# Cross scores of a row's four groups issued as one call over four banks, with the gated loop's order written out by hand

## The chip, the cores and the metric

The program runs on one core of a Trainium2 chip. The time is device time in microseconds, as the median of several executions. The range over which the executions before the change spread is given below, with the profiled execution's own time.

## The reference, cut to what matters

Sixteen rows of 128 tokens with 256 features pass through four layers: a memory layer with a gate, a layer with self attention, cross attention and two experts, and two layers of media attention with feed-forward. The change is in the attention part of the second layer. There each row has 16 heads for self attention (16 features a head, causal) and 16 heads for cross attention (8 features a head, no mask):

```python
def sdpa(q, k, v, causal):
    scale = 1.0 / np.sqrt(q.shape[-1])
    scores = jnp.einsum('bhqd,bhkd->bhqk', q * scale, k)
    ...
    p = jax.nn.softmax(scores.astype(jnp.float32), axis=-1).astype(q.dtype)
    return jnp.einsum('bhqk,bhkd->bhqd', p, v)
ctx = sdpa(q, k, v, causal=True)
hidden_states = residual + jnp.where(vm, ctx @ v_dense, ctx @ l_dense)
ci = rms_norm(hidden_states, ln_post_cross_w)
cctx = sdpa(cq, ck, cv, causal=False)
hidden_states = hidden_states + cctx @ cdense_w
```

## The kernel before, in words

**Units and passes.** The 16 rows are worked in 4 iterations of two units, A (0) and B (1), with two rows each. The second layer's attention is "phase 1". It is software-pipelined: a loop body that runs 3 times (called a pass here) holds the cross attention of this iteration and the self attention of the next. Before the first pass stands a prologue, and after the last one a drain whose order (`ORDER[2]`) is written out, and which overlaps the rounding of the experts' weights.

**Steps.** A step is named kind.attention.unit.row.group, as `scores_cross.cross.0.1.2`; a plus behind it means that it belongs to the next iteration. Every engine walks the same list of steps and runs its own part of each, in order. So a step's place in the list is its place in the queue of each engine that has a part in it. The text writes a step by kind, unit, row and group.

**Softmax of a group.** The 16 heads of a row are four groups of four heads, and the scores of a group (128 by 512) fill one PSUM bank. For one group: TensorE writes the scores, VectorE takes the row maxima (L1511), ScalarE takes the exponential from PSUM to an SBUF buffer with row sums (four activations, each with a read of its accumulator, L1774), VectorE takes reciprocals for two groups (L1518, step `share`), GpSimd multiplies two groups by them (L1994), TensorE transposes (step `turn`, L1021), VectorE copies the transposed bank to SBUF (L1406), and TensorE multiplies by the values (step `mix`, 128x32 column tiles).

**Cross scores.** The contraction of a group is over 32 partitions. One call of `scores_gated` issues two groups, on 32 rows of the array each and on one bank each. Self scores use 64 rows each, also two groups to a call, after two bf16 matmuls that write the causal mask.

**Banks.** All scores of phase 1 share banks 0 to 3, in rotation over the list. A row has four groups, so group g always lies in bank g. The mixes use bank 7, and all other steps (turns, xvT and xlT, qk, v1, dense and so on) rotate over banks 4 to 6. Before TensorE writes a bank it waits in `take` until the step that held it has been emptied. For scores this is the exponential, for xvT and xlT ScalarE's copy, for a turn VectorE's copy. These waits stand in TensorE's queue, and nothing behind one of them starts before it.

**Order.** The loop body's order comes from a table: `gated_slots()` lays the attention steps out in 16 slots, and `gated_sides()` adds the projections. The four score calls of a unit's cross attention stand apart. Between the third (0.1.0) and the fourth (0.1.2) stand both `qk` steps, the longest steps on TensorE in the body.

**Row sums and maxima.** `nmax`, `rsum` and `rshare` have four slots, by group, for both rows.

Of the kernel before, what the change touches and what calls it, by code (L numbers as in the profile page):

```python
# [30 lines left out]
P = 128  # L31
# [95 lines left out]

def gated_slots():
# [19 lines left out]
    for k in range(n):  # L148
        slots.append((of(k - 4, mix) + of(k - 3, lambda *pair: groups_of("turn", pair)),
                      of(k, lambda *pair: groups_of("scores", pair))  # L150
                      + of(k - 1, lambda *pair: groups_of("share", pair)[0:1])))
# [20 lines left out]

def gated_body():
    return [front + first + early + second + late
            for (first, second), (front, early, late) in zip(gated_slots(), gated_sides())]
# [108 lines left out]
def steps_self(norms, pre):  # L284
    slots = gated_body()
    if pre[0] == ("scale_self", A_):
        return [s for slot in slots for s in slot]
# [175 lines left out]
for _i in range(len(PLAN)):  # L463
# [9 lines left out]
        turn_cross.cross.0.0.0 scores_cross.cross.0.1.2 scores_cross.cross.0.1.3 share_cross.cross.0.1.0  # L473
        dense.1.0 round.experts.0 turn_cross.cross.0.0.1 dense.1.1 mix_cross.cross.0.0.0 norm_cross.1
        round.experts.1 turn_cross.cross.0.0.2 turn_cross.cross.0.0.3 split.experts.0 scale_cross.1
        share_cross.cross.0.1.2 mix_cross.cross.0.0.1 ck.1 coT.0.0 round.experts.2 split.experts.1
        turn_cross.cross.0.1.0 turn_cross.cross.0.1.1 nT.1 mix_cross.cross.0.1.0 finish.experts.0
        round.experts.3 turn_cross.cross.0.1.2 spread_cross.1.0 turn_cross.cross.0.1.3 cdense.0.0
        split.experts.2 half.0 mix_cross.cross.0.1.1 coT.0.1 cv.1 finish.experts.1 round.experts.4 cq.1
        spread_cross.1.1 split.experts.3 cdense.0.1 finish.experts.2 end.0 scores_cross.cross.1.0.0 norm_mlp.0  # L480
# [5 lines left out]
        turn_cross.cross.1.0.2 turn_cross.cross.1.0.3 split.experts.6 share_cross.cross.1.1.2 norm_mlp.1  # L486
# [3 lines left out]
        cdense.1.0 finish.experts.8 half.1 round.experts.11 split.experts.10 mix_cross.cross.1.1.1 cdense.1.1  # L490
        coT.1.1 finish.experts.9 end.1 split.experts.11 xvT2.0 xlT2.0 finish.experts.10 finish.experts.11
# [123 lines left out]
def build(nc, dram, out):  # L615
    with ExitStack() as ctx:
# [47 lines left out]
        rsum = sb("rsum", [P, P_RING, QUAD])  # L664
        rshare = sb("rshare", [P, P_RING, QUAD])
        pT_ring = [sb_twin(f"pT{i}", [P, BANK]) for i in range(PT_RING)]
        nmax = sb("nmax", [P, P_RING, QUAD])
# [196 lines left out]
        def settle(eng, name):  # L864

            eng.sem_inc(settled[name], 1)
# [139 lines left out]
        def _(pe):  # L1006
# [99 lines left out]

            def scores_gated(ph, it, s):
# [4 lines left out]
                banks = [ps[ph.bank[s[:4] + (g + i,)]] for i in range(2)]  # L1112
# [290 lines left out]
        def _(dve):  # L1403
# [105 lines left out]
            def scores(ph, it, s, bank):  # L1509
                dve.wait_ge(*after(ph, it, s, "mm"))  # L1510
                dve.tensor_reduce(nmax[:, s[4], :], bank[:, :].rearrange("p (h t) -> p h t", h=QUAD),  # L1511
                                       AX_X, ALU.max, negate=True).then_inc(sems[s[0], "max"], 1)

            def share(ph, it, s, bank):
# [3 lines left out]
                dve.reciprocal(rshare[:, g:g + 2, :], rsum[:, g:g + 2, :]).then_inc(sems[s[0], "rinv"], 1)  # L1518
# [189 lines left out]
        def _(act):  # L1708
# [49 lines left out]
            def scores(ph, it, s, bank):  # L1758
# [13 lines left out]
                for j in range(QUAD):  # L1772
                    part = slice(j * P, (j + 1) * P)
                    t = act.activation(p[:, part], bank[:, part], ACT.Exp, bias=nmax[:, g, j:j + 1],  # L1774
                                       accum_out=rsum[:, g, j:j + 1])
# [146 lines left out]
        def _(pool):  # L1922
# [65 lines left out]
            def share(ph, it, s, bank):  # L1988
# [3 lines left out]
                for n in range(2):  # L1992
                    p = p_of(s[:4] + (g + n,)).rearrange("q (h t) -> q h t", h=QUAD)
                    t = pool.tensor_tensor(p, p, rshare[:, g + n, :].unsqueeze(2).broadcast_to([P, QUAD, P]), ALU.mult)  # L1994
# [103 lines left out]
```

## Time and profile before

| | |
|---|---|
| median of 3 runs | 1407.32 us (1405.79 to 1413.47) |
| the profiled execution's own time | 1406.32 us |
| its span | 1404.1 us |
| what lies around the span | 2.2 us |
| one pass of the gated loop, from 236.88 to 324.97 | 88.09 us |
| TensorE busy in that pass | 86.18 us |
| ScalarE, GpSimd, VectorE busy in it | 57.35, 56.07, 55.85 us |
| the three passes | about 147 to 411 us |
| the drain | about 411 to 476 us |

Times in the profile count from the span's start. Engines: PE is TensorE, PEld its weight loads, DVE is VectorE, ACT is ScalarE, POOL is GpSimd. A float32 matmul is recorded as two matmuls with two weight loads, so two groups of cross scores give four records. A record's end is modelled. What a step costs TensorE is read from its start to the start of the step behind it.

### The profile page before, as it was taken

Reading aid. Unit: us, or ns where it says so; the run is one execution under the profiler, and the core shown is the slowest. Engines: PE = TensorE matmul, PEld = TensorE weight load, DVE = VectorE, ACT = ScalarE, POOL = GpSimd, SP = SyncE. Lnnn points to the kernel's source line nnn. Section 1 sums busy time; section 2 is a strip of 40 time slices with the busy share of each in tenths; the row PEclk is TensorE's granted clock in tenths of the full one; section 3 lists DMA queues with packets and bytes.
Section 4 is the critical chain, followed back from the end, with each engine's and each line's share of the span. In section 5 each row is a group of like instructions: output and inputs, shape, how many; then the busy total and the mean of one; then the engine's idle time right before and its main releaser. Section 6 shows DMA issues by size and latency. Waiting matters only on the chain.

```text
span 1404.1 us, 32336 instructions
## 1 busy us (share of the span) xinstructions
PE 1328.4 (95%) x10898; PEld 1102.9 (79%) x10898; DVE 868.3 (62%) x1837; ACT 755.1 (54%) x2861; POOL 435.8 (31%) x574
## 2 busy tenths in 40 slices
PE   7978999999997899999999999999989999998999
PEld 6844555555554799999888889889988888987999
DVE  4754566666665767548556666566666656556664
ACT  2333676566765722213866666663367665657422
POOL 1354666656664200000132333211013232323000
PEclk9999999999997799999999999999999999999999
DMA  5230000000000200000100000011001000000000
GB/s 180 81 129 4 5 5 5 4 0 4 4 1 1 99 1 0 0 1 1 62 9 5 4 4 4 0 35 64 0 1 65 6 4 4 7 0 1 9 22 30
DMA packets 13928, 30.33 MB, mean 22 GB/s; under 512 B 2832, under 2 KB 9488, under 8 KB 13200
## 3 DMA queue, kind: packets, MB, share of 16 engines
q1 hardware_dynamic: 13840, 29.23, 6.0%
q8 instruction: 46, 0.75, 0.2%
q14 instruction: 42, 0.34, 0.1%
HBM read 27.13 MB, written 2.10 MB: 21 GB/s over the span
## 4 chain that ended last, share of the span: by engine, by line
PE 74%; POOL 7%; DVE 6%; issue 6%; ACT 5%; SPq 1%; DMA 0%; POOLq 0%; DVEq 0%; ACTq 0%
PE bank L1008 65%; PE bank L1021 9%; POOL p L1994 2%; ACT p L1774 1%; POOL xn L1959 1%; DVE stats L1436 1%; POOL o L1994 1%; POOL kbd L1975 1%; DVE pT L1406 1%; DVE nmax L1511 1%; POOL kbd L1985 1%; POOL kbd L1994 1%; ACT kbd L1774 0%; DVE w_ff_rounded L1590 0%; DMA ctxT<-in_ctxT 0%
## 5 line engine op out<-in xcount | busy, mean ns | idle before, releaser
L1511 DVE TENSOR_REDUCE nmax<-bank 128x4 f32<-128x512 f32 x256 | 165.1, 685 | 97.9 <-PE bank L1008 96.7
L1406 DVE COPY pT<-bank 128x512 f32<-128x512 f32 x256 | 164.4, 681 | 90.9 <-PE bank L1021 90.7
L1008 PE MATMUL bank<-w_ff_rounded,hT_rounded 128*128 128x256 f32 x944 | 216.0, 284 | 4.2 <-ACT w_ff_rounded L1901 3.8
L1774 ACT ACTIVATE p<-bank,nmax 128x128 f32<-128x128 f32 x512 | 181.3, 397 | 70.0 <-DVE nmax L1511 69.8
L1994 POOL TENSOR_TENSOR p<-p,rshare 128x512 f32<-128x512 f32 x128 | 132.3, 1054 | 215.7 <-DVE rshare L1518 215.6
L1008 PE MATMUL bank<-xT_rounded,w_ff_rounded 128*128 128x256 f32 x864 | 196.1, 284 | 1.5 <-DVE xn_rounded L1573 1.5
L1008 PE MATMUL bank<-xn_rounded,w_ff_rounded 128*128 128x256 f32 x608 | 172.0, 283 | 0.0
L1008 PE MATMUL bank<-xT_rounded,kbd_rounded 128*128 128x256 f32 x608 | 171.9, 283 | 0.0
L1008 PEld LDWEIGHTS bank<-w_ff_rounded,hT_rounded 128*128 128x128 f32 x944 | 162.2, 191 | 5.4 <-issue 4.2
L1008 PEld LDWEIGHTS bank<-xT_rounded,w_ff_rounded 128*128 128x128 f32 x864 | 148.8, 192 | 2.1 <-DVE xn_rounded L1573 1.7
L1008 PE MATMUL bank<-kbd,hT 64*128 64x128 f32 (+2 forms) x1280 | 144.9, 354 | 4.4 <-ACT p L1774 3.7
L1711 ACT ACTIVATE o<-bank 128x512 f32<-128x512 f32 (+1 forms) x104 | 60.3, 582 | 145.2 <-PE bank L1008 133.2
L1008 PEld LDWEIGHTS bank<-pT,v 128*32 128x32 f32 (+1 forms) x2048 | 79.8, 124 | 66.4 <-issue 26.2
L1008 PE MATMUL bank<-pT,v 128*32 128x128 f32 (+1 forms) x2048 | 113.1, 283 | 18.0 <-DVE pT L1406 8.1
L1774 ACT ACTIVATION_READ_ACCUMULATOR p<-bank,nmax 128x1 f32 x512 | 120.6, 236 | 0.0
L1008 PEld LDWEIGHTS bank<-xn_rounded,w_ff_rounded 128*128 128x128 f32 x608 | 116.6, 192 | 0.0
L1008 PEld LDWEIGHTS bank<-xT_rounded,kbd_rounded 128*128 128x128 f32 x608 | 116.5, 192 | 0.0
L1008 PEld LDWEIGHTS bank<-kbd,hT 64*128 64x128 f32 (+1 forms) x1280 | 88.6, 190 | 26.9 <-issue 25.3
L1774 ACT ACTIVATE kbd<-bank,nmax 128x128 f32<-128x128 f32 x256 | 90.8, 403 | 29.0 <-DVE nmax L1511 29.0
L1008 PE MATMUL bank<-w_ff_rounded,o_rounded 128*128 128x256 f32 x352 | 99.5, 283 | 0.0
L1994 POOL TENSOR_TENSOR kbd<-kbd,rshare 128x512 f32<-128x512 f32 x64 | 65.7, 1047 | 92.8 <-DVE rshare L1518 92.8
L1629 DVE SCALAR_TENSOR_TENSOR x_all<-bank,tgates,x_all 128x256 f32 (+1 forms) x64 | 30.4, 481 | 98.2 <-PE bank L1008 98.1
(182 smaller groups left out, 3128.3 us busy)
## 6 DMA issues: line engine op xcount, KB each, us to landing
ctxT<-in_ctxT SPq DMA_DIRECT2D x32, 128.0 KB, 2.4
w_ff<-in_w1b SPq DMA_DIRECT2D x6, 640.0 KB, 6.4
w_att<-in_w2a SPq DMA_DIRECT2D x1, 3072.0 KB
w_att<-in_w3a SPq DMA_DIRECT2D x1, 3072.0 KB
w_att<-in_w1a SPq DMA_DIRECT2D x1, 2304.0 KB
hT<-in_xT SPq DMA_DIRECT2D x8, 256.0 KB, 3.1
o<-in_x SPq DMA_DIRECT2D x8, 256.0 KB, 2.8
w_ff<-in_w2b SPq DMA_DIRECT2D x1, 2048.0 KB, 7.6
```

Of the source, the lines that this page charges most:

```text
L1008: return pe.matmul(dst, lhsT, rhs, start=first, stop=last)
L1021: t = pe.transpose(bank[:, i * P:(i + 1) * P], src, ident[:])
L1406: dve.tensor_copy(dst, src).then_inc(sems[s[0], "copied"], 1)
L1436: t = dve.bn_stats(stats[:, u, b, :], of(b))
L1511: dve.tensor_reduce(nmax[:, s[4], :], bank[:, :].rearrange("p (h t) -> p h t", h=QUAD), AX_X, ALU.max, negate=True).then_inc(sems[s[0], "m ...
L1629: dve.scalar_tensor_tensor(out=x_b, in0=ps[ph.bank[job]][:, 0:D].unsqueeze(1), scalar=tgates[:, n:n + 1], in1=x_b, op0=ALU.mult, op1=ALU.a ...
L1711: act.activation(dst, src, func, scale=scale).then_inc(sems[s[0], event], 1)
L1774: t = act.activation(p[:, part], bank[:, part], ACT.Exp, bias=nmax[:, g, j:j + 1], accum_out=rsum[:, g, j:j + 1])
L1959: pool.tensor_tensor(xn[u][:, :, :, :], x_all[:, rows(it, u), :].unsqueeze(2).broadcast_to(to_all), rstd_in[:, rows(it, u), :].unsqueeze(3 ...
L1975: pool.tensor_tensor(w.k1[:, b, c, :, :], src.unsqueeze(1).broadcast_to([P, QUAD, P]), rows_self[:, :].unsqueeze(2).broadcast_to([P, QUAD, ...
L1985: pool.tensor_tensor(w.ck1[:, b, :, :], src.unsqueeze(1).broadcast_to([P, QUAD, P]), rows_cross[:, :].unsqueeze(2).broadcast_to([P, QUAD, ...
L1994: t = pool.tensor_tensor(p, p, rshare[:, g + n, :].unsqueeze(2).broadcast_to([P, QUAD, P]), ALU.mult)
```

## The change

1. All four groups of a row's cross scores are issued in one call: TensorE takes banks 0 to 3, one after another, and issues four matmuls on the array's rows 0, 32, 64 and 96. The steps of groups 1 to 3 do nothing on TensorE any more. VectorE and ScalarE still run one step for each group.
2. The loop body is no longer made from the table, but written out in `GATED_BODY`. It holds the same 156 steps in another order.
3. The drain's order `ORDER[2]` is changed at some places. Its cross score calls fall to the place of group 0 as well.
4. `nmax` and `rsum` get eight slots, by row and group. The reciprocal is taken in place, and `rshare` is gone.

```diff
+def scores_of(kind, u, b, c):
+    if kind == "self":
+        return groups_of("scores", (kind, u, b, c))
+    return [("scores_cross", kind, u, b, g) for g in range(GROUPS)] if c == 0 else []
...
+GATED_BODY = """
+    mix.self.1.0.0 scale_self.0+ turn.self.1.0.2 turn.self.1.0.3 scores_cross.cross.0.0.0 mix.self.1.0.1 ctx.1.0
+    scores_cross.cross.0.0.1 scores_cross.cross.0.0.2 scores_cross.cross.0.0.3 turn.self.1.1.0 turn.self.1.1.1
+    share.self.1.1.2 mix.self.1.1.0 xvT.0+ xlT.0+ share_cross.cross.0.0.0 scores_cross.cross.0.1.0
+    scores_cross.cross.0.1.1 scores_cross.cross.0.1.2 turn.self.1.1.2 scores_cross.cross.0.1.3 turn.self.1.1.3
+    qk.0.0+ qk.0.1+ mix.self.1.1.1 share_cross.cross.0.0.2 dense.1.0 ctx.1.1 turn_cross.cross.0.0.0
...
+    scores.self.0.1.1+ coT.0.1 share.self.0.0.2+ turn.self.0.0.0+ turn.self.0.0.1+ cv.1 spread_cross.1.1
+    scores.self.0.1.2+ scores.self.0.1.3+ cq.1 cdense.0.1 share.self.0.1.0+ scale_self.1+ mix.self.0.0.0+ end.0
+    turn.self.0.0.2+ scores_cross.cross.1.0.0 scores_cross.cross.1.0.1 turn.self.0.0.3+ scores_cross.cross.1.0.2
+    scores_cross.cross.1.0.3 share.self.0.1.2+ mix.self.0.0.1+ ctx.0.0+ turn.self.0.1.0+ turn.self.0.1.1+ xvT.1+
+    xlT.1+ mix.self.0.1.0+ share_cross.cross.1.0.0 turn.self.0.1.2+ turn.self.0.1.3+ scores_cross.cross.1.1.0
+    scores_cross.cross.1.1.1 scores_cross.cross.1.1.2 scores_cross.cross.1.1.3 qk.1.0+ qk.1.1+
...
+    cdense.1.0 half.1 coT.1.1 turn.self.1.0.0+ scores.self.1.1.2+ turn.self.1.0.1+ cq.0+ cv.0+
+    scores.self.1.1.3+ cdense.1.1 share.self.1.1.0+ end.1 spread_cross.0.1+"""
...
+            def at_once(s):
+                return GROUPS if s[1] == "cross" else 2
...
-                banks = [ps[ph.bank[s[:4] + (g + i,)]] for i in range(2)]
+                banks = [ps[ph.bank[s[:4] + (g + i,)]] for i in range(at_once(s))]
...
-                    if s[4] % 2 == 0:
-                        take(ph, it, s)
-                        settle(pe, "tensor")
-                        take(ph, it, s[:4] + (s[4] + 1,))
-                        settle(pe, "tensor")
+                    if s[4] % at_once(s) == 0:
+                        for i in range(at_once(s)):
+                            take(ph, it, s[:4] + (s[4] + i,))
+                            settle(pe, "tensor")
...
-                dve.reciprocal(rshare[:, g:g + 2, :], rsum[:, g:g + 2, :]).then_inc(sems[s[0], "rinv"], 1)
+                at = b * GROUPS + g
+                dve.reciprocal(rsum[:, at:at + 2, :], rsum[:, at:at + 2, :]).then_inc(sems[s[0], "rinv"], 1)
```

## Rows read from the trace of the kernel before

**Rows 1.** The page's first two parts: busy time, and the span in 40 slices.

```profile
PE 1328.4 (95%) x10898; PEld 1102.9 (79%) x10898; DVE 868.3 (62%) x1837; ACT 755.1 (54%) x2861; POOL 435.8 (31%) x574
...
PEclk9999999999997799999999999999999999999999
```

**Rows 2.** Busy time by stretch: stretch, its length, each engine's busy time (instructions), granted clock, DMA.

```profile
236.88:324.97 88.09, 86.18 (x613) 49.23 (x612) 55.85 (x117) 57.35 (x292) 56.07 (x60) 1.00 0.01 3
...
412.00:476.00 64.00, 50.53 (x356) 29.81 (x352) 43.08 (x95) 41.72 (x182) 28.87 (x39) 0.73 0.02 6
...
417.30:420.70 3.40, 2.07 (x25) 0.87 (x23) 2.66 (x6) 3.40 (x21) 2.60 (x3) 1.00 0.02 5
...
420.00:430.00 10.00, 10.00 (x54) 4.92 (x55) 4.93 (x10) 6.69 (x38) 4.14 (x5) 0.54 0.00 1
```

**Rows 3.** PE in order of time, a pass's start: start, length, instructions, idle before and releaser.

```profile
238.78 1.13 PE L1008 MATMUL bank<-kbd,hT 32*128 32x512 f32 x4
239.84 0.65 PE L1008 MATMUL bank<-pT,v 128*32 128x128 f32 x16
240.41 1.09 PE L1021 MATMUL bank<-consts,kbd 128*128 128x128 f32 x8
241.91 1.09 PE L1021 MATMUL bank<-consts,xn 128*128 128x128 f32 x8 [0.40 <-POOL xn L1959]
242.93 1.13 PE L1008 MATMUL bank<-kbd,hT 32*128 32x512 f32 x4
244.06 0.64 PE L1008 MATMUL bank<-pT,v 128*32 128x128 f32 x16
244.64 1.09 PE L1021 MATMUL bank<-consts,o 128*128 128x128 f32 x8
245.66 1.13 PE L1008 MATMUL bank<-kbd,hT 32*128 32x512 f32 x4
246.72 7.13 PE L1008 MATMUL bank<-w_att,xT 128*128 128x512 f32 x16
```

**Rows 4.** The same view of DVE.

```profile
236.35 1.29 DVE L1511 TENSOR_REDUCE nmax<-bank 128x4 f32<-128x512 f32 x2 [2.11 <-PE bank L1008]
...
239.91 1.29 DVE L1511 TENSOR_REDUCE nmax<-bank 128x4 f32<-128x512 f32 x2 [0.43 <-PE bank L1008]
```

**Rows 5.** The same view of ACT.

```profile
237.08 0.37 ACT L1774 ACTIVATE o<-bank,nmax 128x128 f32<-128x128 f32 x1 [1.64 <-DVE nmax L1511]
...
239.74 0.24 ACT L1774 ACTIVATION_READ_ACCUMULATOR o<-bank,nmax 128x1 f32 x1
...
243.59 0.42 ACT L1786 ACTIVATE hT<-bank 128x256 f32<-128x256 f32 x1
243.85 1.62 ACT L1741 ACTIVATE xT<-bank,consts 128x256 f32<-128x256 f32 x4
...
246.66 0.47 ACT L1774 ACTIVATE p<-bank,nmax 128x128 f32<-128x128 f32 x1
...
248.03 0.50 ACT L1774 ACTIVATE kbd<-bank,nmax 128x128 f32<-128x128 f32 x1
...
249.40 0.53 ACT L1774 ACTIVATE kbd<-bank,nmax 128x128 f32<-128x128 f32 x1
```

**Rows 6.** The same view of POOL.

```profile
239.96 1.90 POOL L1959 TENSOR_TENSOR xn<-x_all,rstd_in 128x1024 f32 x1
241.81 2.04 POOL L1994 TENSOR_TENSOR o<-o,rshare 128x512 f32<-128x512 f32 x2
```

**Rows 7.** PE in order of time, ahead of the first pass and in the drain.

```profile
146.65 0.59 PE L1008 MATMUL bank<-causal,ident 128*128 128x512 bf16 x2
147.17 1.13 PE L1008 MATMUL bank<-kbd,hT 64*128 64x512 f32 x4
...
149.83 1.13 PE L1008 MATMUL bank<-kbd,hT 32*128 32x512 f32 x4
...
453.34 2.08 PE L1008 MATMUL bank<-kbd,hT 32*128 32x512 f32 x4 [3.71 <-ACT p L1774]
```

**Rows 8.** ACT in the drain, the record that ends an exponential's bank.

```profile
452.83 0.21 ACT L1774 ACTIVATION_READ_ACCUMULATOR p<-bank,nmax 128x1 f32 x1
```

More of the change, by code:

```diff
@@ L149, in gated_slots @@
         slots.append((of(k - 4, mix) + of(k - 3, lambda *pair: groups_of("turn", pair)),
-                      of(k, lambda *pair: groups_of("scores", pair))
+                      of(k, scores_of)
                       + of(k - 1, lambda *pair: groups_of("share", pair)[0:1])))
@@ L173, in gated_body, with step @@
 def gated_body():
-    return [front + first + early + second + late
-            for (first, second), (front, early, late) in zip(gated_slots(), gated_sides())]
+    def step(text):
+        return tuple(int(x) if x.isdigit() else x for x in text.rstrip("+").split("."))
+    return [[(step(text), int(text.endswith("+"))) for text in GATED_BODY.split()]]
 def media_slots():
@@ L285, in steps_self @@
     slots = gated_body()
-    if pre[0] == ("scale_self", A_):
+    if ("scale_self", A_) in pre:
         return [s for slot in slots for s in slot]
@@ L489 @@
         finish.experts.7 turn_cross.cross.1.1.2 round.experts.10 turn_cross.cross.1.1.3 split.experts.9
-        cdense.1.0 finish.experts.8 half.1 round.experts.11 split.experts.10 mix_cross.cross.1.1.1 cdense.1.1
-        coT.1.1 finish.experts.9 end.1 split.experts.11 xvT2.0 xlT2.0 finish.experts.10 finish.experts.11
+        cdense.1.0 finish.experts.8 xvT2.0 xlT2.0 half.1 round.experts.11 split.experts.10 finish.experts.9
+        mix_cross.cross.1.1.1 cdense.1.1 coT.1.1 end.1 split.experts.11 finish.experts.10 finish.experts.11
         round.experts.12 round.experts.13 split.experts.12 round.experts.14 split.experts.13 finish.experts.12
@@ L663, in build @@
         p_ring = [sb_twin(f"p{i}", [P, BANK]) for i in range(P_RING)]
-        rsum = sb("rsum", [P, P_RING, QUAD])
-        rshare = sb("rshare", [P, P_RING, QUAD])
+        rsum = sb("rsum", [P, ROWS * GROUPS, QUAD])
         pT_ring = [sb_twin(f"pT{i}", [P, BANK]) for i in range(PT_RING)]
-        nmax = sb("nmax", [P, P_RING, QUAD])
+        nmax = sb("nmax", [P, ROWS * GROUPS, QUAD])
         rows_self = sb("rows_self", [P, QUAD])
@@ L1510, in scores @@
                 dve.wait_ge(*after(ph, it, s, "mm"))
-                dve.tensor_reduce(nmax[:, s[4], :], bank[:, :].rearrange("p (h t) -> p h t", h=QUAD),
+                dve.tensor_reduce(nmax[:, s[3] * GROUPS + s[4], :], bank[:, :].rearrange("p (h t) -> p h t", h=QUAD),
                                        AX_X, ALU.max, negate=True).then_inc(sems[s[0], "max"], 1)
@@ L1773, in scores @@
                     part = slice(j * P, (j + 1) * P)
-                    t = act.activation(p[:, part], bank[:, part], ACT.Exp, bias=nmax[:, g, j:j + 1],
-                                       accum_out=rsum[:, g, j:j + 1])
+                    t = act.activation(p[:, part], bank[:, part], ACT.Exp, bias=nmax[:, b * GROUPS + g, j:j + 1],
+                                       accum_out=rsum[:, b * GROUPS + g, j:j + 1])
                 t.then_inc(sems[s[0], "exp"], 1)
```

31 lines of the change are left out of this document (22 added, 9 removed).

## The prediction

> **What bounds the kernel now.** I read the page first: TensorE is busy 95% of the span [rows 1], so an instruction saved there can count. Then busy time by stretch, for the stage that the change touches. In one pass of the gated loop TensorE works 86.18 of 88.09 us, and no other engine more than 57.35 [rows 2]. The pass is bound by TensorE's queue, with little waiting. The three passes take 3 x 88.1 = 264 us of 1404. The drain is another matter: TensorE is busy 50.53 of 64.00 us, and the granted clock is 0.73 on average [rows 2], so latency between engines sets its time. Then I read each engine in order of time to price steps and chains [rows 3 to 8]. The reader should look for starts: the step behind a cross score call starts 1.06 us after it (238.78 to 239.84, 245.66 to 246.72).
>
> **What is removed on TensorE.** Two groups of cross scores cost 1.06 us. One record of a 512-column float32 matmul costs TensorE 0.44 (16 records in the 7.0 us of the two qk steps [rows 3]). Four in turn would be 1.8, so the two groups already run side by side, and what is paid is one group's two records (0.87) plus 0.2 for filling and draining the array at the change of tile. If four groups run as two do, the call costs hardly more: I take 1.07. Bounds: 1.06 if the other two are free, 2.12 if the array takes them two by two.
>
> A pass has eight calls before and four after, so 4 x 1.05 = 4.2 us go. Where the neighbours of a removed call are both 128-row work, they now follow without a drain of the array. A turn of four transposes takes 0.49 behind another kind of tile and 0.44 behind its own kind. Summing all steps of a pass by their start-to-start distances, those of rows 3 and like ones for the rest, and leaving waits out, gives 84.9 us before and 80.2 after: **-4.7 us a pass**. The pass before thus has 88.1 - 84.9 = 3.2 us of waits. Two of its waits are for xn from GpSimd (0.40 in rows 3, at 241.91).
>
> If all waits stayed as they are, the passes would give 3 x 4.7 = 14 us back.
>
> The Trainium skill, "TensorE: Matmul & The Clock Gate", Part 3, gives a measured speedup of 3.07 for four row tiles of 32 rows with 512 columns. By it, as an estimate, the call would take (4 x 0.87 + 0.2) / 3.07 = 1.2 us, and the calls would save 3.6 us a pass, not 4.2. No run here shows four tiles yet.
>
> **What is added: a wait for all four banks.** A call with two groups needs two banks empty, and the other two may still be in ScalarE's hands. A call with four needs all of them. Only ScalarE's last exponential frees bank 3. So between two calls of a unit lies the full latency of four exponentials. I walk it from the first call's start, Q:
> - VectorE's first maximum starts at Q + 1.13 (238.78 to 239.91 [rows 3, 4]).
> - ScalarE's first exponential starts 0.73 later (236.35 to 237.08 [rows 4, 5]), at Q + 1.9. The maxima come every 0.6 us (two in 1.29 [rows 4]), faster than ScalarE uses them.
> - One bank's exponentials take 1.37 us from start to start (246.66, 248.03, 249.40 [rows 5]), and the last ends about 1.5 after its start. Two banks took 237.08 to 239.98. Four end at Q + 1.9 + 3 x 1.38 + 1.5 = Q + 7.5.
> - The new order puts ctx.1.0 between the first and second (0.26 from start to start, 243.59 to 243.85 [rows 5]): Q + 7.8.
> - TensorE needs another 0.3 us through its waits once the bank is free: in the drain an exponential's last record ends at 453.04 [rows 8], and the call that waited for it starts at 453.34, after 3.71 us of idling [rows 7]. This is the wait that now comes into the loop.
>
> So unit A's second call can't start before **Q + 8.1**. What TensorE has to do between the two calls in the new list is the first call, mix, two turns, mix, xvT and xlT: 1.07 + 0.58 + 1.02 + 0.58 + 1.02 = 4.3 us. **Wait: 3.8.** The 7.0 us of qk, which could cover it, stand behind the call. Within these 3.8 us one wait is only moved: VectorE takes four maxima ahead of the copies of turns 1.1.0 and 1.1.1, so the mix behind them starts at Q + 5.0 and not Q + 2.7.
>
> Unit B's second call: the four exponentials end at R + 7.5, then come in ScalarE's queue ctx.0.0 (0.26) and xvT.1's two copies (0.8 to 0.9, half of 243.85 to 245.28 [rows 5]), at R + 8.6. Turn 0.1.3 stands ahead of the call and takes the bank that xvT.1 held, so it starts at 8.7, and the call at R + 9.2. TensorE's work between is 5.7. **Wait: 3.5.**
>
> Unit B's first call waits for self group 0.1.3 and then for cq.1's copy, which the new list puts behind it on ScalarE. From the start of the self call 0.1.2: 0.53 for the mask [rows 7], 1.13 to the maximum, 0.73 to the exponential, 1.38 + 1.5 for two banks, 0.45 for cq's copy, 0.3 to start: 6.0. TensorE's work between is 4.2. **Wait: 1.8.** Unit A's first call waits for self group 1.1.3, whose exponential stands behind the copies of cq.0 and cv.0: it ends 5.9 us after its call's start, so the wait, 0.3 to start included, is **0.5** over 5.6 us of work.
>
> The rest of the pass I walked in the same way. Four small waits come out: dense.1.1 for its bank from dense.1.0 (0.3), ck.1 for that of turn 0.1.0 (0.4), turn 1.1.3 for nT.0's (0.2), and self call 1.1.2 for GpSimd's spread (0.2). GpSimd's shares of 2.04 us and its xn of 1.90 [rows 6] arrive in time, because the waits at the calls give it time.
>
> Sum of waits: 3.8 + 3.5 + 1.8 + 0.5 + 1.1 = 10.7 us against 3.2, **+7.5 a pass**. Net of the work saved: **+2.8 a pass, +8.3 in three**. The walk has some 60 joints. I give it 1.5 us a pass to either side.
>
> "TensorEngine Tiling (Array Packing)" of the Trainium skill, Performance Considerations, says that tiling speeds TensorE but not the emptying of PSUM, which may then bound. By that rule the saving would shrink. The rows above put ScalarE in that place, in two stretches of a pass only: over the whole pass it is 57 of 88 us busy.
>
> **Into the first pass.** Before, the first cross call starts 3.2 us after self call 1.1.2 (146.65 to 149.83 [rows 7]), with two banks long free. After, it waits for the exponential of 1.1.3, at + 5.9: **+2.7**. No earlier step has the slack to give this back, since the prologue's steps hang on each other.
>
> **The drain.** Four calls fewer at half clock (2.08 each [rows 7]) are 8 us of TensorE's work, but its time is set by the chain of exponentials. Unit A: the first call comes 1.9 us later (it waits for 1.1.3), and the last exponential some 1.8 earlier, as it no longer waits for the fourth call. Unit B: 3.71 us of idling stood before the third call already, and it grows by two exponentials, while the fourth call's wait goes. I take **0**, from -3 to +2. The moved steps of `ORDER[2]` go by at most three places, and their work (a copy or a rounding of 0.4 to 0.7 us) lies beside these waits.
>
> **The clock.** From 417.3 to 420.7 TensorE was busy 2.07 of 3.40 us, with waits for ScalarE. After this the granted clock was half (1.2 GHz in place of 2.4) for most of 420 to 430 [rows 2]. In the three passes it was never below full. After the change, TensorE works some 1.6 of the 5.5 us up to unit A's second call, and about half of a like stretch in unit B. So I expect the clock to fall about once a pass. While it is low, the work (turns, the call, a part of qk) takes double. Bounds: 0, and 3.5, if in both units a quarter of the 7 us of qk behind the second call still runs at half clock. I take 1.2 a pass, **+3.6**, since a part of each lies in the waits.
>
> **nmax, rsum and the reciprocal in place** change addresses. The reciprocals (0.2 us) stay as many. A maximum that had to wait for a slot would show here, but no wait of that kind stood in the code. Cost: 0. No DMA is added or moved: the queue on SP waits for cv and ck of the same pass, with nearly a pass of room.
>
> **Sum.** 8.3 + 2.7 + 0 + 3.6 = +14.6 on the profiled execution's own 1406.3 (span 1404.1) gives 1420.9. The median shown is 1 us above it. I round down to **1420**, as the clock's share is the least sure.
>
> **The rivals.**
> - *The work saved comes through (0.19).* If ScalarE frees the four banks in time, waits stay at about 3 us a pass, and the time is 1406 - 14 - 2 = **1390**. For it: 95% TensorE, 20 to 30 us of slack a pass on the others. Against: it needs four exponentials within 4.3 us, where four take 5.6. It decides itself at unit A's second call: if it starts before Q + 5.5, this rival holds.
> - *Saving and waits cancel (0.10).* My walk is 2 us a pass too dark, as some waits get covered, and the clock holds: **1408**, within 1401 to 1414.
> - *Four tiles don't run side by side (0.07).* The call then takes 2.1. As all four calls start late, most of the 1.05 us each is added: 12 passes' calls and 4 in the drain, some +14 over the forecast: **1434**.
> - *The forecast (0.64)*, with its own range of 1411 to 1429. One sixth of it lies below 1414.4.
>
> **How the numbers follow.** Half a per cent, 7 us, is about what a measurement of this kernel can tell from no change: 1400.3 and 1414.4 are the bounds. Faster: 0.18, nearly all of the first rival. Same: 0.20, the second rival and the lower edge of the forecast. Slower: 0.62. The range goes from 1396, inside the faster rival's upper tail, to 1431, short of the fourth case.
>
> **What the profile after would show.** Four-group calls of 1.07 us from start to start, with eight records. A PE idle time before unit A's second call (together with the mix before it) of 3 to 4 us, put down to ScalarE's exponential. From first to second call about 8.1 us in A and 9.2 in B. A pass of about 91 to 92 us with TensorE busy some 81, and half-clock stretches in it. I would be wrong if a pass is under 88 us: then look whether the second call starts before its row's third bank has been emptied, or the exponentials run faster than 1.37 us a bank.

## The result, and the profile after

The changed kernel takes 1428.35 us in the median (1425.35 to 1429.98, 4 runs), beside 1408.97 us for the kernel before (1405.79 to 1413.47, 4 runs): a ratio of 1.016 with a 95% interval of 1.0122 to 1.0197 (the quotient of the two medians alone is 1.014). It is slower, by 19 us between the medians and 24 between the two profiled executions. The forecast was 1420 us, within 1396 to 1431: the sign and the range hold. The size does not: 14.6 us were added up for the profiled execution, and it lost 23.7. The profiled execution took 1429.98 us, span 1427.8.

The page's first two parts answer to [rows 1]:

```profile
PE 1318.5 (92%) x10898; PEld 1106.1 (77%) x10898; DVE 874.6 (61%) x1837; ACT 756.5 (53%) x2861; POOL 434.3 (30%) x574
...
PEclk9989999999999799999999999999999999999999
```

TensorE is busy 10 us less than before, and the kernel takes 24 us more. Busy time by stretch, as in [rows 2]: the three passes of the gated loop, each from unit A's first cross call to the next, and the drain up to the first matmul of the MLP.

```profile
154.01:247.95 93.94, 83.38 (x612) 48.96 (x613) 57.70 (x117) 57.84 (x292) 55.97 (x61) 0.98 0.01 4
247.95:344.05 96.10, 85.94 (x612) 50.62 (x613) 57.70 (x117) 57.84 (x292) 55.96 (x61) 0.95 0.01 3
344.05:439.79 95.74, 86.11 (x612) 51.19 (x613) 57.60 (x117) 57.84 (x292) 55.87 (x61) 0.95 0.01 2
439.79:498.09 58.30, 37.52 (x327) 24.52 (x327) 41.03 (x92) 39.57 (x167) 26.10 (x37) 0.82 0.00 1
```

A pass took 88.1 us and takes 94 to 96, and the granted clock, 1.00 in a pass before, is 0.95 to 0.98. The starts of the same TensorE steps in the two traces split the 23.7 us of span:

| part | before | after | difference | forecast |
|---|---|---|---|---|
| start of the first cross call | 149.83 | 154.01 | +4.2 | +2.7 |
| three passes | 265.0 | 285.8 | +20.8 | +8.3, and +3.6 for the clock |
| drain, to the MLP's first matmul | 61.5 | 58.3 | -3.2 | 0 |
| the rest of the kernel | 927.8 | 929.7 | +2.0 | 0 |

TensorE in order of time, the second pass's start (it answers to [rows 3]), and below the dots unit B's calls in the same pass:

```profile
247.95 1.14 PE L1046 MATMUL bank<-kbd,hT 32*128 32x512 f32 x8 [0.57 <-ACT o L1816]
249.02 0.64 PE L1046 MATMUL bank<-pT,v 128*32 128x128 f32 x16
249.60 1.09 PE L1059 MATMUL bank<-consts,kbd 128*128 128x128 f32 x8
252.86 0.64 PE L1046 MATMUL bank<-pT,v 128*32 128x128 f32 x16 [2.17 <-issue]
253.44 1.50 PE L1059 MATMUL bank<-consts,xn 128*128 128x128 f32 x8
256.25 2.09 PE L1046 MATMUL bank<-kbd,hT 32*128 32x512 f32 x8 [1.31 <-ACT p L1816]
258.27 1.97 PE L1059 MATMUL bank<-consts,o 128*128 128x128 f32 x8
...
296.80 1.14 PE L1046 MATMUL bank<-kbd,hT 32*128 32x512 f32 x8 [1.50 <-ACT hT L1753]
...
299.87 0.64 PE L1046 MATMUL bank<-pT,v 128*32 128x128 f32 x16 [1.34 <-DVE pT L1447]
...
304.76 0.74 PE L1046 MATMUL bank<-pT,v 128*32 128x128 f32 x16 [2.15 <-ACT hT L1828]
305.43 1.97 PE L1059 MATMUL bank<-consts,o 128*128 128x128 f32 x8
307.33 1.74 PE L1046 MATMUL bank<-kbd,hT 32*128 32x512 f32 x8
```

Three things are to be seen. The call of four groups has eight records and costs 1.07 us (247.95 to 249.02), what the call of two cost. TensorE now idles ahead of three of the four calls and ahead of the mixes between two calls. The releasers are ScalarE's exponentials and copies in four of these six waits, VectorE's copy in one (299.87), and none is named in one (252.86). And at 256.25 the work takes about double: the same call 2.02, the record of the two turns behind it 1.97 in place of 1.09.

ScalarE in order of time, the first and the last exponential between unit A's two calls, answers to [rows 5]:

```profile
249.89 0.37 ACT L1816 ACTIVATE p<-bank,nmax 128x128 f32<-128x128 f32 x1 [2.32 <-DVE nmax L1552]
...
255.31 0.46 ACT L1816 ACTIVATE p<-bank,nmax 128x128 f32<-128x128 f32 x1
255.56 0.30 ACT L1816 ACTIVATION_READ_ACCUMULATOR p<-bank,nmax 128x1 f32 x1
```

From Q, the start of unit A's first call (247.95), the first starts at Q + 1.94, the last ends at Q + 7.91, and the call starts 0.39 later, at Q + 8.30. The walk had 1.9, 7.8 and 8.1.

VectorE in order of time (it answers to [rows 4]) shows the other wait:

```profile
249.08 2.48 DVE L1552 TENSOR_REDUCE nmax<-bank 128x4 f32<-128x512 f32 x4 [0.81 <-PE bank L1046]
251.48 1.28 DVE L1447 COPY pT<-bank 128x512 f32<-128x512 f32 x2
```

Four maxima stand ahead of the copies of the two turns. The mix that needs these copies starts at 252.86, Q + 4.9 (the walk: 5.0), and the profile names no releaser for its 2.17 us.

### The profile page after: what moved, and what is told of

Its sections match the earlier page's. It is cut to its first block, busy times and chain, and to the rows that moved or that the text cites. A ratio compares the mean times of both kernels' runs of the same rounds, so it can differ in the third digit from the quotient of the medians.

```text
span 1427.8 us, 32323 instructions
## 1 busy us (share of the span) xinstructions
PE 1318.5 (92%) x10898; PEld 1106.1 (77%) x10898; DVE 874.6 (61%) x1837; ACT 756.5 (53%) x2861; POOL 434.3 (30%) x574
## 4 chain that ended last, share of the span: by engine, by line
PE 75%; ACT 9%; DVE 8%; issue 4%; POOL 2%; SPq 1%; DMA 0%; DVEq 0%; ACTq 0%; POOLq 0%
PE bank L1046 66%; PE bank L1059 9%; ACT p L1816 4%; DVE nmax L1552 2%; ACT o L1816 1%; DVE stats L1477 1%; DVE pT L1447 1%; ACT kbd L1816 1%; DVE x_all L1582 1%; DMA ctxT<-in_ctxT 0%; ACT v L1753 0%; DVE w_ff_rounded L1632 0%; POOL kbd L2017 0%; POOL rstd L1983 0%; SPq L969 0%
## 5 line engine op out<-in xcount | busy, mean ns | idle before, releaser
L2036 POOL TENSOR_TENSOR p<-p,rsum 128x512 f32<-128x512 f32 x128 | 132.3, 1054 | 211.6 <-DVE rsum L1560 211.6
L1046 PE MATMUL bank<-kbd,hT 64*128 64x128 f32 (+2 forms) x1280 | 128.0, 363 | 17.9 <-ACT p L1816 11.2
L1046 PEld LDWEIGHTS bank<-kbd,hT 64*128 64x128 f32 (+1 forms) x1280 | 84.6, 193 | 38.1 <-issue 36.5
L2036 POOL TENSOR_TENSOR kbd<-kbd,rsum 128x512 f32<-128x512 f32 x64 | 65.8, 1048 | 83.9 <-DVE rsum L1560 83.7
```

Source lines behind the costliest of these rows:

```text
L1046: return pe.matmul(dst, lhsT, rhs, start=first, stop=last)
L2036: t = pool.tensor_tensor(p, p, rsum[:, s[3] * GROUPS + g + n, :].unsqueeze(2).broadcast_to([P, QUAD, P]), ALU.mult)
```

## The experiments

All are timed beside the kernel before on the same chip. Its medians there were 1407.45 us (12 runs) for the first four experiments, 1406.45 (31 runs) for the next four, 1403.0 (29 runs) for the three tries further, and 1408.39 (13 runs) for the last. The ratios and intervals given are not quotients of two medians. Pass lengths are from unit A's first call to the next.

**The order alone.** The changed kernel, with calls of two groups.

```diff
             def at_once(s):
-                return GROUPS if s[1] == "cross" else 2
+                return 2
```

> The changed kernel with its new order, but cross score calls of two groups again. Theory (waits for the banks, and the clock falls that they bring): the new list puts the two calls of a row side by side, so the call for groups 2 and 3 of the second row still waits for the first row's last exponential, 8.1 us after the first call. TensorE does 4.2 us more work a pass, most of it inside these waits: 1421 to 1430 us, a pass of 93 to 96 us. Rival (the four-group call itself is slow on the array or on the banks): the time falls clearly, to 1412 or less, since that call is gone.

1414.55 us (1413.60 to 1418.80, 9 runs), ratio 1.0069 (1.0044 to 1.0095). A pass is 92.1 us, with the clock low for 6.8 us in it; the drain is 52.9. The number lies between the two expectations, and the wait that was expected for the last call hardly shows: it starts 8.26 us after the first call, after an idle time of 0.13 us only. The new order costs the loop 4 us a pass by itself. TensorE is busy 87.76 of the 92.11 us, so 2.4 us of the 4 are more waits than before (4.35 against 1.9), and 1.6 are work at half clock. The maxima still stand ahead of the turns' copies (the mix waits 1.57 us), and the copies ahead of unit B's call (1.5). The calls of four add 3.2 us a pass to that.

**Calls of four alone.** The calls of four in the lists of the kernel before, for the loop and the drain.

```diff
-GATED_BODY = """ ... """
 def gated_body():
+    return [front + first + early + second + late
+            for (first, second), (front, early, late) in zip(gated_slots(), gated_sides())]
```

> Calls of four groups, with the loop's and the drain's order of the kernel before. Theory (waits for the banks): in the old order the second call of a unit stands even nearer, and the copies of xvT and xlT stand between the exponentials, so it starts 9.6 us after the first, over 5.2 us of work, and the first call of a unit waits for the last self exponential (1.8). Pass 95 us without and 97 with falls of the clock: 1428 to 1440 us. Rival (the new order is at fault, not the call of four): the work saved shows, 1390 to 1400 us.

1439.98 us (1437.02 to 1442.28, 4 runs), ratio 1.0251 (1.0195 to 1.0306); a pass of 99.0. TensorE's waits in the second pass (total, times, longest):

```profile
PE bank L1043 <- ACT p L1813: 5.8, 2, 2.9
PE bank L1043 <- ACT o L1813: 5.0, 3, 1.8
PE bank L1043 <- ACT hT L1825: 2.7, 2, 1.4
PE bank L1043 <- ACT hT L1832: 0.8, 2, 0.4
```

In the same order with calls of two, TensorE's waits in a pass were these:

```profile
PE bank L1021 <- POOL xn L1959: 1.1, 2, 0.7
PE bank L1008 <- ACT hT L1793: 0.8, 2, 0.4
```

None was for an exponential; now they are 10.8 us of a pass. The time lies at the upper edge of what was expected, and the pass is 2 us longer than the 97 expected. So the wait comes with the calls of four, and the new order takes off some of it: of the four combinations the pass is 88.1 (old, two), 99.0 (old, four), 92.1 (new, two), 95.3 (new, four, mean of three).

**The clock.** The changed kernel, with transposes repeated into a bank that the turn holds anyway, so that TensorE works where it waited. They add 52 transposes a pass and leave the results as they are.

```diff
+            AGAIN = {("turn", "self", 1, 1, 0): 2, ("turn", "self", 1, 1, 1): 1, ("xlT", 0): 4,
+                     ("turn", "self", 0, 0, 3): 1, ("xlT", 1): 5}
...
+                    for i, src in blocks_and_places:
+                        pe.transpose(bank[:, i * P:(i + 1) * P], src, ident[:])
```

> The changed kernel, where in the passes TensorE repeats transposes of five turns inside its waits (same data, same bank, before anybody is told). It adds 5.7 us of TensorE's work a pass, in places where it idles, so as to keep the clock up. Theory (the falls of the clock cost 3 to 4 us a pass): no or few stretches at half clock in the passes, and 1417 to 1422 us. Rival (the low clock falls into waits and costs nearly nothing): the clock stays up, and the time stays within 3 us of 1428, or grows if the added work delays a copy.

1420.09 us (1419.37 to 1420.27, 4 runs), ratio 1.0109 (1.0057 to 1.0162). Busy time of the second pass:

```profile
244.09:336.40 92.31, 87.37 (x665) 53.94 (x665) 57.62 (x117) 57.71 (x292) 55.91 (x61) 1.00 0.01 3
```

TensorE does more, and the kernel is 8.3 us faster than the changed one by the medians. These were taken beside two different runs of the kernel before, whose medians differ by 1.5 us, so 7 to 8 us are safe. The clock is full in all three passes, and they take 92.3 us each: 276.8 in all, 8.9 less than in the changed kernel. The distance from first to second call is 8.28 in unit A, as before the repeats, so it was not the clock that set that one; in unit B it is 9.55, where it was 10.1 to 10.8.

**A copy earlier in unit B.** mix.self.0.0.1 and ctx.0.0 stand right behind turn 0.0.3, so that ScalarE's copy does not stand behind four exponentials.

```diff
-    ... turn.self.0.0.3+ scores_cross.cross.1.0.2 scores_cross.cross.1.0.3 share.self.0.1.2+ mix.self.0.0.1+ ctx.0.0+ ...
+    ... turn.self.0.0.3+ mix.self.0.0.1+ ctx.0.0+ scores_cross.cross.1.0.2 scores_cross.cross.1.0.3 share.self.0.1.2+ ...
```

> The changed kernel with one move: unit B's mix.0.0.1 and ctx.0.0 stand before groups 2 and 3 of its first row, so ScalarE copies ctx.0.0 between the second and third exponential and not behind the fourth. Theory (the mix of row 1 waits for this copy, as all mixes hold bank 7, and pushes the second call from 9.2 to 10.5 us behind the first): the second call comes at 9.2 us, the pass loses 1.3 to 2 us, and the time is 1422 to 1425. Rival (the second call is held by the exponentials and the xvT copy alone): no change, 1427 to 1429.

1421.68 us (1421.23 to 1424.38, 4 runs), ratio 1.0121 (1.0069 to 1.0173). The time comes out just under what was expected, and for another reason. The wait of 2.15 us at 304.76 is gone, but one of 1.48 us for a copy of xT stands a step later, and the second call still starts 9.5 us after the first, as in the run of the repeated transposes. What the run gains on the changed kernel is clock. Its first two passes:

```profile
152.57:244.98 92.41, 82.18 (x613) 48.28 (x613) 57.72 (x117) 57.84 (x292) 55.50 (x61) 1.00 0.01 4
244.98:340.51 95.53, 85.33 (x612) 49.66 (x613) 57.72 (x117) 57.84 (x292) 55.96 (x61) 0.96 0.01 3
```

Same list, same code: 92.4 us at full clock and 95.5 with 6.8 us at half. This gives the clock's price a second time, and without added work.

**The second call behind qk.** In the changed kernel's list unit A's second call is placed behind qk.0.0 and unit B's behind qk.1.0, and the copies ctx, xvT, xlT between the first and the second exponential. Some neighbours move too: the shares, the turns ahead of the second calls, and in unit B the self call 0.1.2, which now stands ahead of turn.0.0.0. The cut shows unit A.

```diff
-    share.self.1.1.2 mix.self.1.1.0 xvT.0+ xlT.0+ share_cross.cross.0.0.0 scores_cross.cross.0.1.0 ...
-    qk.0.0+ qk.0.1+ ...
+    ... xvT.0+ xlT.0+ scores_cross.cross.0.0.1 scores_cross.cross.0.0.2 scores_cross.cross.0.0.3 mix.self.1.1.0 ...
+    share_cross.cross.0.0.0 qk.0.0+ scores_cross.cross.0.1.0 ... scores_cross.cross.0.1.3 qk.0.1+ ...
```

> The changed kernel with its calls of four, but in the loop's list the second cross call of unit A stands behind the step qk.0.0 and that of unit B behind qk.1.0 (3.5 us of TensorE's work each, now between the two calls in place of behind them); share.1.1.2, ctx, xvT and xlT are placed so that ScalarE's queue holds fewer copies between the exponentials. Theory (the calls of four save their work, and only the wait for four exponentials ate it): the work between the calls is now 7.8 us or more, so the waits of 3.8 and 3.5 us go and with them the falls of the clock; a pass of 85 to 87 us, 1396 to 1404 us in all. Rival (ScalarE's exponentials cost their time wherever the call stands, and their lateness only shows at the next step): the pass stays at 91 us or more and the time at 1412 or more.

> The same move as in the run before, in unit A alone; unit B as in the changed kernel. Theory: unit A's wait of some 4 us goes and unit B's stays. 3.5 us of work are now under the exponentials in each of three passes, and the falls of the clock at unit A (about 1.2 us a pass) go too: a pass of 90 to 92 us and 1412 to 1417 us in all, half of the way to the run with both. Rival (the wait moves from A to B's call, as a pass has one fixed total of latency): as the changed kernel, 1425 or more.

Both units: 1407.72 us (1406.21 to 1408.86, 10 runs), ratio 1.0003 (0.9984 to 1.0022). Unit A alone: 1414.92 us (1413.76 to 1415.37, 10 runs), ratio 1.0059 (1.0039 to 1.0078). The second is as expected. The first falls between the two expectations: all of the loss is gone, and no gain comes. Busy time of its second pass, and TensorE in order of time:

```profile
240.22:328.42 88.20, 82.36 (x612) 48.05 (x613) 57.65 (x117) 57.45 (x292) 56.01 (x61) 1.00 0.01 3
```

```profile
243.98 0.64 PE L1046 MATMUL bank<-pT,v 128*32 128x128 f32 x16
244.86 1.09 PE L1059 MATMUL bank<-consts,o 128*128 128x128 f32 x8 [0.24 <-POOL o L2036]
245.79 3.60 PE L1046 MATMUL bank<-w_att,xT 128*128 128x512 f32 x8
249.97 1.14 PE L1046 MATMUL bank<-kbd,hT 32*128 32x512 f32 x8 [0.58 <-ACT p L1816]
```

The mix of 2.17 us's wait has none now, since one maximum and not four stands ahead of its copies, and the second call waits 0.58 in place of 1.31, at full clock. But the call starts 9.75 us after the first (240.22), not 8.3: ScalarE now has xT's copies too, 1.4 us, among the four exponentials. TensorE is busy 3.8 us less than in the pass before (86.18 [rows 2]) and waits 3.9 us more (5.8 against 1.9): saving and waits cancel.

**Short exponentials.** One instruction of ScalarE for each cross bank. It leaves out each head's own maximum and three of the four row sums.

```diff
+                if kind == "cross":
+                    t = act.activation(p[:, :], bank[:, :], ACT.Exp, scale=0.001, accum_out=rsum[:, at, 0:1])
-                for j in range(QUAD):
+                for j in range(QUAD if kind != "cross" else 0):
```

> The changed kernel with its list, but each cross group is exponentiated by one ScalarE instruction of 512 columns in place of four of 128 (without each head's own maximum, and with one row sum where there are four: this leaves a part of the computation out). This shortens only ScalarE's part of the chain that empties the banks, from 1.37 us a bank to an estimated 0.6. Theory (the four exponentials set the second call): the second call starts at about Q + 5.3 in unit A, where VectorE's four maxima now set it, in place of Q + 8.3; a pass of 85 to 88 us; with a shorter drain too, 1385 to 1400 us in all. Rival (the wait is not ScalarE's but the turns' and copies' on VectorE, or the taking of four banks one by one): first to second call stays at 7.5 us or more and the pass at 91 or more.

1401.7 us (1399.59 to 1405.32, 10 runs), ratio 0.9972 (0.9945 to 0.9999); a pass of 88.6. Both are a little above what was expected, and clearly below the rival's 91 us a pass. TensorE in order of time:

```profile
241.08 1.14 PE L1046 MATMUL bank<-kbd,hT 32*128 32x512 f32 x8 [0.57 <-ACT o L1819]
...
245.99 0.64 PE L1046 MATMUL bank<-pT,v 128*32 128x128 f32 x16 [2.17 <-issue]
246.56 1.09 PE L1059 MATMUL bank<-consts,xn 128*128 128x128 f32 x8
247.59 1.14 PE L1046 MATMUL bank<-kbd,hT 32*128 32x512 f32 x8
```

With ScalarE's part short, the second call comes 6.5 us after the first (8.3 in the changed kernel, 5.3 expected) and waits for nothing, and the clock stays full in all three passes. The mix waits its 2.17 us as before, so that wait is VectorE's four maxima and not an exponential. Two causes stand one behind the other here, and the walk had both.

**Eight slots alone.** The kernel before, with the new nmax and rsum and the reciprocal in place.

> The kernel before, with only the change of nmax and rsum to eight slots and the reciprocal written in place. Theory: no cost and no gain, 1404 to 1411 us, as forecast (0). Rival (the four slots shared by two rows made VectorE or GpSimd wait): some us faster, 1400 or less.

1408.76 us (1400.63 to 1411.25, 10 runs), ratio 1.0017 (0.9988 to 1.0046); a pass of 88.05. No cost that can be told from nothing, as forecast.

**Three tries further.** To the second calls behind qk, mix.self.1.1.1 and mix.self.0.1.1 moved ahead of the second calls and dense.0.1 moved back; then the drain in calls of two with that; and the new list of the drain in the kernel before.

```diff
-    ... qk.0.0+ scores_cross.cross.0.1.0 ... qk.0.1+ mix.self.1.1.1 ...
+    ... qk.0.0+ mix.self.1.1.1 scores_cross.cross.0.1.0 ... qk.0.1+ ...
```

```diff
-            def at_once(s):
-                return GROUPS if s[1] == "cross" else 2
+            def at_once(s, it):
+                return GROUPS if s[1] == "cross" and not isinstance(it, int) else 2
```

> The kernel with the second calls behind qk.0.0 and qk.1.0 (pass 88.2 us, of it 5.9 us of waits), with three steps moved more: mix.self.1.1.1 and mix.self.0.1.1 between qk and the second call (0.58 us of work each, where that call still waits 0.58 and 0.67 us), and dense.0.1 behind mix_cross.1.0.0 (it waits 1.36 us for a copy of ScalarE). Theory (a call of four costs nothing once as much work as four exponentials take stands between two calls): about 2.5 us of waits go, a pass of 85.7 us and 1397 to 1404 us in all, faster than both kernels. Rival (a pass has 8 us of latency that only moves from wait to wait): pass 88 or more, 1406 or more.

> The same, but the drain behind the loop takes its cross scores in calls of two. There is no qk to stand between two calls there: unit B's second call waited 7.0 us. The run of calls of two with the new order had a drain of 52.9 us from the first call to the first matmul of the MLP, against 56.4 with calls of four and 61.5 in the kernel before. Theory: the drain takes 53 us, 3.5 us less than with calls of four: 1393 to 1401 us in all. Rival (the drain's time is the order's and not the calls'): no difference to the run before this one.

> The loop and the calls of two of the kernel before; only the new list of the drain (and the eight slots for maxima and sums). Theory (forecast before: the moved steps of the drain are worth nothing, since they lie beside waits): no change, 1404 to 1410 us, with the drain at 61 us. Rival (the new list is what made the drain shorter): drain of 53 to 55 us, 1398 to 1403 us in all.

The first took 1408.91 us (1406.58 to 1415.80, 12 runs), ratio 1.0042 (1.0015 to 1.0069), where 1397 to 1404 was expected: a miss. Its second pass is 88.2 us, no shorter. TensorE in order of time:

```profile
247.65 3.60 PE L1046 MATMUL bank<-w_att,xT 128*128 128x512 f32 x8
251.18 0.64 PE L1046 MATMUL bank<-pT,v 128*32 128x128 f32 x16
252.38 1.14 PE L1046 MATMUL bank<-kbd,hT 32*128 32x512 f32 x8 [0.55 <-issue]
```

The mix took 0.58 us of work out of the wait, and the call came 10.3 us after the first in place of 9.75. The last exponential's record ends at 251.43, so 0.95 us pass before the call; behind qk it was 0.39. dense.0.1 waited 1.35 us at its new place too. The pass has 6.0 us of waits, where it had 5.8. The rival holds: the waits moved.

The second took 1405.3 us (1402.49 to 1410.01, 12 runs), ratio 1.0011 (0.9987 to 1.0036), 3.6 us below the first, the 3.5 that were expected; the level is missed with that of the first. The drain is 52.9 us in its profile and 58.3 in that of the first, so the calls of four do lengthen it in this list.

The third, the kernel before with the new drain, took 1406.68 us (1397.96 to 1411.05, 12 runs), ratio 1.0004 (0.9979 to 1.0029). Yet the drain in its profile is 52.2 us, against 61.5 in that of the kernel before:

```profile
412.95:465.18 52.23, 38.34 (x327) 22.90 (x327) 41.93 (x93) 40.85 (x176) 26.55 (x38) 0.89 0.00 1
```

To see whether the drain's length is the list's or the execution's, the kernel before was profiled once more.

> The kernel before, unchanged, profiled once more. The run with only the new drain had a drain of 52.2 us in its profile (61.5 in the profile of before, 62.8 in that of the eight slots) but a median no lower than that of before. Theory (the drain's length differs between executions of one kernel, through where the clock falls): this profile shows a drain other than 61 us by some microseconds, or an own time near 1398 with a drain under 57. Rival (the new list does shorten the drain by 9 us, and something else takes it back): a drain of 60 to 63 us in this profile too.

```profile
413.76:476.57 62.81, 47.33 (x328) 28.09 (x327) 41.21 (x92) 40.42 (x174) 27.72 (x38) 0.74 0.03 7
```

1407.7 us (1399.42 to 1411.36, 10 runs), ratio 0.9991 (0.9966 to 1.0016): the measure of no change. The drain came out as the rival had it. Three profiles of the old list with calls of two have drains of 61.5, 62.8 and 62.8 us, and three of the new list with calls of two 52.9, 52.9 and 52.2. The granted clock in them is 0.72 to 0.74 and 0.89. But this does not show that the list shortens the drain. The three profiles of the old list were taken in executions of 1406 to 1411 us, and that of the new list in the same loop in one of 1398, the fastest of its twelve. Both kernels have executions of both kinds: under 1403 us lie 14 of the 29 of the kernel before in that session, and 4 of the 12 with the new list. The other two profiles of the new list, in executions of 1407.6 and 1414.3 us, speak for the list, but their loops differ. No execution of the kernel before near 1398 us was profiled, so this rival stands.

## Why the forecast had the sign right and the size too small

The step that failed is a term that was mis-sized: **the clock**. The prediction said "I expect the clock to fall about once a pass" and took "1.2 a pass, +3.6". In the changed kernel's three passes it was half for 3.4, 10.2 and 10.2 us (0.98, 0.95 and 0.95 on average over the stretches shown). The three take 285.8 us, and three passes at full clock take 3 x 92.3 = 276.9 (the repeated transposes; the moved copy's first pass says 92.4): **8.9 us, not 3.6**. The bound had been 3.5 a pass; the second and third pass lost 3.8 and 3.4. The value had one fall a pass. But each unit's second call has a clump of waits ahead of it, and five of these six clumps in the three passes had a fall: one in the first pass, two in each of the others. The reason given for the value, that part of the slow work lies in waits, holds for unit A alone. There the clock is low from 253.98 to 260.8, and the call starts at 256.25, so 2.3 of these 6.8 us end in the call's wait and cost nothing. The call, the two turns and the start of qk behind it have no wait to hide in (busy time by stretch, the changed kernel):

```profile
254.00:260.80 6.80, 5.49 (x22) 3.18 (x21) 2.47 (x5) 4.99 (x26) 2.99 (x3) 0.50 0.00 0
...
301.80:305.20 3.40, 1.25 (x22) 0.79 (x20) 0.80 (x3) 3.40 (x19) 3.40 (x4) 1.00 0.01 2
305.20:308.60 3.40, 3.40 (x24) 2.09 (x16) 1.38 (x2) 0.97 (x3) 0.03 (x1) 0.50 0.00 0
```

The last two show unit B: TensorE works 1.25 of 3.4 us while the mix ahead of the second call waits for ScalarE, busy all of it, and then runs at 1.2 GHz in place of 2.4 when the turns and the second call come. The first pass had a fall in unit B only, 3.4 us long, and lost 1.6 us by it: nearly all of it fell on work. The 276.9 us are an estimate from the two other kernels, since the changed kernel has no pass at full clock; its first pass, less half of the 3.4 us, gives 92.2 too.

**The waits.** TensorE's waits in the second pass of the changed kernel, by releaser (total, times, longest):

```profile
PE bank L1046 <- issue: 2.2, 1, 2.2
PE bank L1046 <- ACT hT L1828: 2.2, 1, 2.2
PE bank L1046 <- ACT hT L1753: 1.5, 1, 1.5
PE bank L1046 <- DVE pT L1447: 1.3, 1, 1.3
PE bank L1046 <- ACT p L1816: 1.3, 1, 1.3
PE bank L1046 <- ACT o L1816: 0.6, 1, 0.6
PE bank L1046 <- DVE x_all L1582: 0.4, 1, 0.4
PE bank L1046 <- ACT hT L1835: 0.4, 1, 0.4
PE bank L1059 <- POOL kbd L2036: 0.2, 1, 0.2
```

Forecast +8.3 in three passes, net of the work saved; measured 276.9 - 265.0 = **+11.9**, the second term that was mis-sized. The walk's single waits are nearly right. Unit A: 3.8 forecast, 2.17 + 1.31 = 3.48 by the rows. Unit B's second: 3.5 against 1.34 + 2.15 = 3.49. Its first: 1.8 against 1.50. Unit A's first: 0.5 against 0.57. The small ones: 1.1 against some 1.0. They add to 10.0 us, where 10.7 was forecast. What was too large is the saving: TensorE's busy time in a pass at full clock goes from 86.18 [rows 2] to 82.18 (the moved copy's first pass), **4.0 us and not 4.7**. And the waits of before, by the same rows, were 1.9 and not 3.2. The 84.9 us of floor that the prediction made of start-to-start distances lie below the busy time that the view gives, so 1.3 us that are no wait were counted as one, and as replaceable. 4.0 less work and 8.2 more waits make +4.2 in the second pass for the forecast +2.8.

**Four tiles side by side.** Right: 1.07 us, and the four row tiles' first records start 7 ns apart. By the 3.07 of the Trainium skill ("TensorE: Matmul & The Clock Gate", Part 3) it would have been an estimated 1.2 us; the trace is 0.13 us below that.

**Into the first pass.** +2.7 forecast, +4.2 measured. From self call 1.1.2 to the first cross call it is 6.25 us in the changed kernel, where it was 3.2: +3.1, the forecast and the 0.3 us to start that the prediction counted at unit A's call and left out here.

```profile
147.76 0.59 PE L1046 MATMUL bank<-causal,ident 128*128 128x512 bf16 x2 [0.69 <-ACT p L1816]
```

The other 1.1 us lie ahead of that step. How much of them is the clock's is not shown: it fell at 103 and 141 us in the prologue before, and at 97 and 107 us in that of the changed kernel. The first cross call starts at 148.0 to 151.0 in the four profiles with the old list and calls of two, and at 151.7 to 155.6 in the eight with a new list in the loop and calls of four.

**The drain.** Forecast 0, measured -3.2, just outside the bounds of -3 to +2. The two profiles can't say why, since executions of one kernel differ here by more. The calls of four cost it 3.6 us by the medians of the two runs that differ in them alone, and the prediction had them at 0. With the drain's old list they cost nothing that shows: 60.5 us in the profile with calls of four, 61.5 to 62.8 in those with calls of two. That the moved steps of `ORDER[2]` are worth nothing, since they "lie beside these waits", is borne out by the times (1.0004, from 3 us less to 4 us more). By the profiles the new list's drain is 9 to 10 us shorter, and that is the open point below.

**How it adds up.** The profiled execution lost 9.1 us more than the sum had: 5.3 by the clock in the passes, 3.6 by waits and saving, 1.5 ahead of the first pass and 2.0 behind the drain, less 3.2 in the drain.

**The slots, and the rest.** The slots cost nothing, as said. Outside the loop and the drain the profile is 2.0 us longer; over the 14 profiles of this study, with the code there the same, that part takes 927.8 to 933.3 us, so this is an execution's chance. That the forecast's range held is partly such chance too, as the drain gave back 3.2 us that were not foreseen.

**What fell.** "The work saved comes through" was to be told at unit A's second call: Q + 8.3, where Q + 5.5 was its point. "Four tiles don't run side by side" fell with the 1.07 us, and "Saving and waits cancel" with the passes of 94 to 96 us. With the second calls behind qk they do cancel. "TensorEngine Tiling (Array Packing)" of the Trainium skill, Performance Considerations, which lets the emptying of PSUM bound what tiling saves, agrees with the trace: ScalarE is busy 57.8 of 96 us only, and yet 5.9 of the 10.0 us of waits end with it by name.

**What stays open.** The drain is 9 to 10 us shorter in the profiles with the new list, and yet the times of the kernel before with it are no better. Why is not shown. In that session both kernels run from 1397 to 1411 us, and their time goes with the mean granted clock in the same way: 0.989 at 1398, 0.978 at 1411. As an estimate, 0.01 less of clock over 1400 us is 28 us more at half clock. The drains of 62.8 and 52.2 us differ by some 21 us of half clock (0.74 and 0.89). So an execution of the kernel before near 1398 us could have the short drain as well. No view here shows one. Nor is it shown what the waits of 5.8 us that remain with the second calls behind qk are bound by together.

## What to carry to other kernels

A call that takes more banks at once also waits for the last of them, so price it by the chain that empties all of them (here one maximum, four banks of exponentials at 1.37 us, and the copies queued among these) against the work that stands between two calls, and count what one engine's larger batch does to the copies behind it. If the bound engine begins to idle in clumps, price its clock apart, as the work behind each clump times two, near its upper bound (here 8.9 us of 10.5). And take saved work from the view of busy time, before and after, rather than from a floor made of start-to-start distances. Before you put a shorter stretch down to your edit, look whether the two profiled executions are alike in time and granted clock.

## What the runs showed of the hardware

- Work added to TensorE made the kernel faster: 52 float32 transposes a pass, in its waits, hold the granted clock at full in all three passes (0.98, 0.95 and 0.95 without them), and the median is 1420.1 us and not 1428.4. "TensorE: Matmul & The Clock Gate" of the Trainium skill, Part 4, says that a transpose doesn't count as busy for the clock in the same way; these float32 ones kept it up.
- The clock is not a function of the list alone: one pass of an execution took 92.4 us at full clock and the next, of the same code, 95.5, with 6.8 us at half.
- Executions of one kernel differ by 1%, and the granted clock with them: the kernel before took from 1397.3 us (0.991) to 1411.2 us (0.978) in one session.
- After the last semaphore of a call with four banks, TensorE starts 0.39 us later where turns (in the changed kernel) or long matmuls (qk, 512 columns) stand ahead of it, and 0.95 us later behind a mix of sixteen short ones, with 0.55 us that nothing in the profile releases. That TensorE's sequencer works off the call's waits in that time was not tried.
